# Diagonal steps ahead of the split of e, and Gram results formed from the first chunk to the third

## What is computed

```python
q = heads(hidden_states @ W_q)
probs_t = softmax(q @ heads(text_ehs @ W_k) * attn_scale)
text_out = probs_t @ heads(text_ehs @ W_v)
qsem = l2norm(einsum('bhst,bte->bhse', probs_t, text_ehs))
sem = einsum('bhse,bne->bhsn', qsem, l2norm(ip_ehs))
probs_ip = softmax(q @ heads(ip_ehs @ W_k_ip) * attn_scale + SEM_SCALE * sem) * spatial_mask
out = (text_out + probs_ip @ heads(ip_ehs @ W_v_ip)) @ W_out + b_out + hidden_states
```

## Time and profile before

| | us |
|---|---|
| median of 3 runs | 390.13 |
| lowest and highest | 387.19, 395.4 |
| the profiled execution | 389.0 |
| its span, first to last instruction | 387.0 |
| TensorE busy in it | 358.2 |
| mean granted TensorE clock | 0.974 of full |

### The profile page before, as it was taken

How to read it: one execution, slowest core, us unless ns; L and a number is a source line. 1 busy time by engine, 2 the same in 40 slices (tenths; PEclk the granted TensorE clock), 3 DMA queues, 4 the chain that set the end, 5 groups by cost and what they waited for, 6 DMA issues and landing times.

```text
span 387.0 us, 9366 instructions
## 1 busy us (share of the span) xinstructions
PE 358.2 (93%) x3498; PEld 304.9 (79%) x3498; DVE 269.1 (70%) x566; ACT 215.7 (56%) x490; POOL 213.1 (55%) x230
## 2 busy tenths in 40 slices
PE   8999799995899979999899979998999899999886
PEld 7879599874788868888788878886888678877664
DVE  4897673693667695587858685687758587867464
ACT  6734133783557455647556554757455458557741
POOL 8020271397138861596438662696349615865872
PEclk9999999998799989999999989999999999999899
DMA  8999993259105802265205702283203710002001
GB/s 265 313 240 188 249 188 105 64 169 157 23 1 158 155 13 59 81 142 103 75 5 176 134 22 65 82 179 63 77 3 103 128 42 3 2 3 58 0 3 31
DMA packets 30145, 38.01 MB, mean 98 GB/s; under 512 B 14394, under 2 KB 27307, under 8 KB 29419
## 3 DMA queue, kind: packets, MB, share of 16 engines
q1 hardware_dynamic: 29732, 37.00, 41.1%
q10 hardware_dynamic: 368, 0.41, 0.3%
HBM read 28.49 MB, written 8.81 MB: 96 GB/s over the span
## 4 chain that ended last, share of the span: by engine, by line
PE 64%; DVE 16%; DMA 9%; issue 6%; SPq 3%; ACT 1%; POOL 0%; DVEq 0%; ACTq 0%
PE PR L1127 32%; PE Y L1127 18%; PE O L1127 7%; PE P L1127 5%; DVE mx L1001 4%; DMA qst<-ma 3%; DVE dl L974 3%; DMA tri<-tri_d 2%; DMA big<-xT 2%; DVE pb L1025 2%; DVE ssq L885 1%; DMA kd<-ks 1%; PE PR L1326 1%; DVE cTl L1101 1%; SPq L519 1%
## 5 line engine op out<-in xcount | busy, mean ns | idle before, releaser
L633 POOL TENSOR_TENSOR pb<-pb 128x448 f32<-128x448 f32 x78 | 91.2, 1170 | 99.9 <-DVE pb L1025 96.9
L1001 DVE TENSOR_REDUCE mx<-PR 112x1 f32<-112x371 f32 x160 | 81.6, 536 | 50.5 <-PE PR L1127 49.5
L1025 DVE TENSOR_TENSOR pb<-big,Y 128x448 f32<-128x448 f32 x120 | 73.5, 617 | 32.1 <-PE Y L1127 30.5
L813 ACT ACTIVATE big<-P 128x448 f32<-128x448 f32 x120 | 64.7, 539 | 55.0 <-PE P L1127 55.0
L1127 PE MATMUL Y<-er,Gh 128*128 128x448 f32 x240 | 93.4, 413 | 1.7 <-ACT er L817 1.4
L817 ACT ACTIVATE er<-big 128x448 fp32r<-128x448 f32 x120 | 69.4, 578 | 3.8
L1127 PE MATMUL P<-qst,kst 99*128 99x112 bf16 x480 | 44.0, 218 | 9.4 <-DMA qst<-ma 9.0
L1127 PEld LDWEIGHTS Y<-er,Gh 128*128 128x128 f32 x240 | 46.1, 192 | 8.0 <-issue 2.3
L1127 PE MATMUL PR<-kst,qst 96*112 96x371 bf16 x160 | 48.7, 329 | 2.5 <-DVE mx L1001 2.1
L1127 PEld LDWEIGHTS P<-qst,kst 99*128 99x128 bf16 x480 | 30.6, 101 | 25.1 <-issue 17.8
L1127 PE MATMUL Y<-er,Gl 128*128 128x448 f32 x120 | 44.4, 370 | 0.0
(11 more groups left out here) (208 smaller groups left out, 719.1 us busy)
## 6 DMA issues: line engine op xcount, KB each, us to landing
et<-ctxT SPq DMA_DIRECT2D x7, 752.0 KB, 4.9
kst<-kd SPq DMA_DIRECT2D x7, 720.0 KB, 7.4
kd<-ks SPq DMA_DIRECT2D x16, 288.0 KB, 2.9
qst<-qd SPq DMA_DIRECT2D x48, 70.0 KB, 3.5
kst<-kd SPq DMA_DIRECT2D x7, 480.0 KB, 9.5
kst<-kd SPq DMA_DIRECT2D x9, 240.0 KB, 9.1
qd<-kst SPq DMA_DIRECT2D x4, 336.0 KB, 7.8
vx<-xr SPq DMA_DIRECT2D x8, 140.0 KB, 2.5
```

Of the source, the lines that this page charges most:

```text
L633: pool.tensor_tensor(total, total, (pz, pm)[j], ALU.add).then_inc(s_S, 1)
L813: act.activation(e, P[(3 * g + c) % 2][:, 0:448], ACT.Exp).then_inc(s_exp, 1)
L1001: dve.tensor_reduce(mx[b % 2][:, h:h + 1], bank[0:S, 0:T], AX.X, ALU.max).then_inc(s_free[seq[u] % NR], 1)
L1025: dve.tensor_tensor((pz, pm, pa[g % 2])[j], eb[g % 3][:, 448 * j:448 * j + 448], Y[y % 2][:, 0:448], ALU.mult).then_inc(s_P, 1)
```

## The change

The order of the words, and what goes with it. Grams run 0, 1, 2: each waits for its own chunk of `er`, the product of gram 0 goes to `pa`, and GpSimd adds after grams 1 and 2. In the middle batches `E` is cut in `Ea` and `Eb`, which stand behind `g1`, so that GpSimd takes gram 1's addition ahead of `el`; `g2` stands behind `o`. In `LATE`, `D` follows `pT`, and `S0` stands behind `cT` and `L`. In the start, `D` and `L` of batch 0 come behind the first maxima. `wo` and `Kr` of batch 0 come one and two rounds sooner; `D` of batch 1 ends round 3 instead of standing in round 4.

```diff
-ROUNDS = ("K0 S0 m g2 m g1 S1 m K1 m S2 m g0 v G0",
-          "S0 m g2 g1 m S1 m g0 K2 C v m S2 G1 m",
-          "S0 m g2 T0 T1 g1 m g0 r0 S1 m pw S2 m v V0 m",
-          "Kr r1 m g2 g1 S0 m m g0 V1 S1 m m S2 v r2 mT z GV",
-          "p g2 pT E g1 D cT S0 S1 v g0 L o S2")
-SECOND = "S0 K0 m g2 g1 m S1 m g0 K1 m v S2 m G0"
-NO_K = "m m S0 g2 m g1 v g0 S1 S2 m m G0"
-EARLY = ("m S1- m S2- K1 S0 m g2 g1 S1 m m g0 m S2 K2",
-         "S0 m g2 g1 S1 m g0 S2 m v m m wo C",
-         "S0 m g2 g1 m S1 g0 m m S2 v m",
-         "Kr S0 m S1 m g2 m g1 m v g0 S2 mT GV",
-         "E g2 g1 S0 g0 D v S1 S2 L")
-LATE = "p g2 pT g1 S0 g0 D cT S1 L S2 v o"
-LAST = ("S0 S1 v g2 S2 g1 T0 T1 g0",
-        "S0 r0 g2 g1 pw v S1 g0 pv S2",
-        "S0 r1 g2 S1 r2 g1 g0 S2 v",
-        "S0 g2 S1 z g1 p g0 S2 v",
-        "pT T0' pw' r0' g2 cT g1 g0 r1' v vW T1' r2' pv'")
+ROUNDS = ("K0 m S0 m g0 g1 S1 m K1 S2 m g2 m v G0",
+          "g0 S0 m m g1 g2 S1 m m K2 C v S2 G1 m",
+          "Kr S0 m g0 m T0 T1 g1 g2 S1 r0 pw m S2 m v V0",
+          "m g0 g1 S0 m r1 m m g2 V1 S1 m S2 m v r2 mT z GV",
+          "p g0 pT g1 Ea Eb D cT S0 S1 v L S2 o g2")
+SECOND = "K0 S0 m K1 g0 g1 m S1 m v g2 m S2 m G0"
+NO_K = "m m S0 S1 g0 m g1 v m g2 S2 m G0"
+EARLY = ("m S1- m S2- K1 S0 g0 g1 S1 m S2 m g2 K2 m wo",
+         "m m g0 S0 g1 S1 m g2 S2 m v m m C Kr",
+         "g0 S0 m g1 m S1 g2 m m S2 v m",
+         "S0 m S1 g0 m m g1 m v g2 S2 mT GV D",
+         "Ea Eb g0 g1 v S0 S1 g2 S2 L")
+LATE = "p g0 pT D g1 g2 cT L S0 S1 v S2 o"
+LAST = ("S0 v g0 S1 g1 T0 g2 S2 T1",
+        "g0 r0 S0 g1 v pw S1 g2 pv S2",
+        "r1 S0 S1 g0 g1 r2 g2 S2 v",
+        "S0 g0 S1 g1 z p S2 g2 v vW",
+        "pT T0' g0 r0' pw' cT g1 g2 r1' v T1' r2' pv'")
@@ master_schedule, the start
-    order += [("D", 0)]
-    side = [("V", 0, 1), ("L", 0), ("V", 0, 2)] + [("qip", b) for b in range(B)]
+    side = [("V", 0, 1), ("D", 0), ("V", 0, 2), ("L", 0)] + [("qip", b) for b in range(B)]
@@ master_schedule, the words
-                elif w == "E":
-                    order += split(b + 3) if b + 3 < B else []
+                elif w in ("Ea", "Eb"):
+                    order += split(b + 3)[2 * (w == "Eb"):][:2] if b + 3 < B else []
@@ GpSimd
-                if u[0] == "gram" and u[2] < 2 and u[1] < NG * B - 1:
+                if u[0] == "gram" and u[2] and u[1] < NG * B - 1:
                     g, j = u[1], u[2]
                     total = pa[g % 2]
-                    pool.wait_ge(s_P, 3 * g + 3 - j)
-                    if j == 0:
+                    pool.wait_ge(s_P, 3 * g + j + 1)
+                    if j == 2:
                         pool.wait_ge(s_S, 2 * g + 1)
-                    pool.tensor_tensor(total, total, (pz, pm)[j], ALU.add).then_inc(s_S, 1)
+                    pool.tensor_tensor(total, total, (pm, pz)[j - 1], ALU.add).then_inc(s_S, 1)
@@ VectorE
-                    y = 3 * g + 2 - j
+                    y = 3 * g + j
                     dve.wait_ge(s_gram, y + 1)
-                    if j == 2 and g >= 2:
+                    if j == 0 and g >= 2:
                         dve.wait_ge(s_pv, g - 1)
-                    if j < 2 and g:
-                        dve.wait_ge(s_S, 2 * g - j)
-                    dve.tensor_tensor((pz, pm, pa[g % 2])[j], eb[g % 3][:, 448 * j:448 * j + 448], Y[y % 2][:, 0:448],
+                    if j and g:
+                        dve.wait_ge(s_S, 2 * g - 2 + j)
+                    dve.tensor_tensor((pa[g % 2], pm, pz)[j], eb[g % 3][:, 448 * j:448 * j + 448], Y[y % 2][:, 0:448],
                                       ALU.mult).then_inc(s_P, 1)
@@ TensorE
-                    y = 3 * g + 2 - j
+                    y = 3 * g + j
                     if y >= 2:
                         pe.wait_ge(s_P, y - 1)
-                    if j == 2 and r == 0:
+                    if j == 0 and r == 0:
                         pe.wait_ge(s_wd, b + 1)
-                    if j == 2:
-                        pe.wait_ge(s_er, 3 * g + 3)
+                    pe.wait_ge(s_er, 3 * g + j + 1)
```

More of the change, by code:

```diff
@@ L125, in master_schedule @@
                 if w == "g":
-                    order += [("gram", g, j) for j in (2, 1, 0)]
+                    order += [("gram", g, j) for j in range(3)]
                 elif w in ("g2", "g1", "g0"):
```

## The result

| | before | after |
|---|---|---|
| median, us | 389.68 | 371.02 |
| lowest and highest | 387.19, 395.4 | 370.6, 371.63 |
| the profiled execution | 389.0 | 370.6 |
| its span | 387.0 | 368.6 |
| TensorE busy | 358.2 | 352.1 |

A forecast was written before the change was run, and what follows sets the result against it. TensorE, busy for 93% of the span, was taken as the bound, leaving waits and lost clock to win. 4.5 + 3.4 + 2.3 + 2.0 + 0.4 + 1.2 - 0.5 = 13.3 us, so 377 us for the median, range 370 to 386.

The forecast's parts named there:

- the likeliest case: Whole kernel: the gains come as summed, 377 us, with its own range 371 to 382; chance 0.65.
- What bounds it, and `el`: Round 4, batches 1 to 4: `el` behind the diagonal steps removes the wait for `cTl` before `o`, 6.86 us.
- Given back to `St`: Batches 1 to 4: `St` chunk 0 waits for `ma` with less cover, 0.6 us lost each, between 0 and 0.8.
- The clock: Batches 1 to 4: two stretches of half clock behind waits before `o` go, 3.4 us, bounds 0 and 3.4.
- Batches 5 and 6: Late order: `St` chunk 0 behind gram 2, `cT` and `L` shortens its wait; 2.3 us, bounds 1.0 and 2.6.
- The start: Batch 0's start: three reductions go ahead of `D`, which waited for `tri`; 2.0 us, bounds 0 and 3.0.
- Batch 0: Batch 0: the earlier `wo` split lets the k load and `ma` start sooner; 0.4 us, bounds -0.5 and 1.5.
- Batch 7 and the grams: Last batch: with grams first to third, gram 2's 1.37 us wait for `er` shrinks; 1.2 us, bounds 0 and 2.9.
- `el` later: Batches 1 to 4: `el` ends later, close to K's need; 0.5 us lost in all, bounds 0 and 4 x 0.8.
- (a): Rival: the wait moves to `St` chunk 0, the clock falls as often, the start gives nothing; 383.7 us, chance 0.22.
- (b): Rival: GpSimd's queue is the limit, its second addition comes last and `pv` waits for it; 387 us, chance 0.08.
- (c): Rival: slower than before, `el` meets `L`'s two instructions, K waits and the clock falls; 391 us, chance 0.05.

The follow-up runs named there:

- a_late_back: The changed kernel with the old order of words in `LATE` (batches 5 and 6), grams first to third; median 374.0 us, ratio 0.958 to the kernel before.
- a_el_ahead: The changed kernel with `el` put back ahead of gram 1 in round 4, all else kept; median 383.7 us, ratio 0.980 to the kernel before.
- b_start: The kernel before with only the start changed, `D` and `L` of batch 0 behind the first maxima; ratio 0.992 to the kernel before.
- a_same: The changed kernel again, unaltered, on another chip; 371.08 us, ratio 0.953 to the kernel before.
- b_gram_up: The kernel before with only the grams turned, `g0` and `g2` changing places in every string of words; ratio 1.021 to the kernel before, 8 us slower.
- a_last_back: The changed kernel with the old words of `LAST` in batch 7, grams first to third; median 373.3 us, ratio 0.959 to the kernel before.
- a_plus: The changed kernel with three more words moved, gram 1 in round 2 of middle batches, `K2` and gram 1 in batch 0; median 372.5 us, ratio 0.955.

## Why the prediction was right, point by point

The measured 371.0 lies inside the range of 370 to 386, but 1 us above its low end and at the edge of the 371 to 382 of the likeliest case; the single value was 377. The main mechanism, `el` beside the diagonal steps, was right. The range held although several terms were off, and with little more than 1 us of gain on top it would not have held.

**What bounds it, and `el`.** Right, and near to the tenth. I gave the diagonal steps 1.97 us, they took 1.96; `cTl` was to end 7.0 us behind `mT` and ended 7.03 behind it; the whole wait in front of `o` went. Moving `el` alone, and moving it back alone, both show that this is the cause.

**Given back to `St`: the step was wrong.** I took 0.6 us in each batch, because `St` chunk 0 waits for `ma` behind the k load. After, `St` starts 5.24 to 5.34 us behind `mT` in batches 1 to 4 and never waits. I had taken the k load's place as fixed, since moving `Kr` does nothing in these batches. That sentence was right, but K's own products come sooner in the new order of round 1: in batch 3 the load was issued 217.81 - 211.54 = 6.3 us ahead of `mT`, and 208.32 - 200.34 = 8.0 after:

```profile
200.34 1.27 SPq L419 DMA_DIRECT2D kst<-kd  x3
...
208.97 2.47 SPq L518 DMA_DIRECT2D qst<-ma  x3
```

A queue that never waits for TensorE still follows the instruction that feeds it. The writes of k were issued 10.6 us ahead of `mT` before and 11.9 after. The sooner load isn't the whole of it: in batch 2 it was issued 6.6 us ahead of `mT` after, and `St` did not wait, where in batch 4 before it was issued 6.7 us ahead and `St` waited until 6.3 us behind `mT`. What else lets `ma` land sooner stays open. The term was 2.4 us too large.

**The clock.** The mechanism is right: fill the waits with matmuls and the clock stays up. The size was the larger miss. I counted the two stretches of batches 1 to 4, 3.4 us, and those came through. I put the clock at nothing in the start, in batch 0 and in batch 7. In the profiled executions all but 3.4 of the 20.5 us at half clock went, and TensorE's busy time fell by 6.1 us. The rule by which I chose, that waits of 1.4 us leave the clock alone, was drawn from two cases. In a_late_back a wait of 1.38 us had half clock behind it; in a_el_ahead one of 1.86 had none, in b_start those of 1.96 and 2.05 had none, and of the 2.52 and 2.80 us in batch 0 of the changed kernel the longer, in a_same, had none. So the length of the last wait alone doesn't decide it. What else does stays open; with less idle time in all there were fewer stretches.

**Batches 5 and 6.** 2.3 us forecast, and 2.5 measured up to `mT` 7, for batch 5 alone; batch 6's share lies in the last column, where its wait of 0.55 us went. Undone, it costs 3.

**The start.** 2.0 us forecast, 2.8 in the profiled execution, 2.2 in b_start and 1.6 in a_same. VectorE is indeed the limit afterwards, and directly only 1.1 us came through; the rest is the half clock at 46.7 and the moment at which the clock first rose. That the term came out near is in part luck.

**Batch 0.** 0.4 us forecast, 2.5 measured. The load was to start up to 1.5 us sooner and I took 0.8 of it; by the timelines it was issued 88.17 - 84.40 = 3.8 us ahead of `mT` before and 5.9 after, 2.2 sooner, and with it the wait fell by 2.8 us. Here, too, the step that failed is that K's products were taken to stay in place: the writes of k were issued 8.9 us ahead of `mT` before and 10.2 after.

**Batch 7 and the grams.** 1.2 us forecast, some 2 measured, for another reason than mine. I had it that gram 2's wait for `er` goes, and that turning the grams costs nothing in the middle, its work being the same. b_gram_up shows that the turn alone costs 8 us, half clock included. a_last_back, turned but with the old words, loses the 2 us again, 1.5 of them by half clock, which I had left out of the term. That the change as a whole did not pay for it I got right without seeing why.

**`el` later.** 0.5 us forecast, nothing measured. `el` was to end 10.7 us behind `mT` and ended 10.05 behind it; K came 9.57 behind it and read the second half in time. The rule of the Trainium skill on VectorE and GpSimd ("SBUF — State Buffer", "Who interferes with whom") agrees with the trace in what it would do here: the first of `L`'s two instructions takes 2.11 us instead of 0.59. It costs nothing where nothing waits, as after, and 1.5 us in four batches where three maxima do, as in a_plus.

**The rivals.** (a), the wait moves, did not come: `St` never waited in batches 1 to 6, and the clock did not fall as often. (b) and (c) did not come either. b_gram_up is near to (b), but the queue that was too slow was VectorE's, with its products, and not GpSimd's.

**The sum by stages.** Forecast against measured, in us: the start 2.0 and 2.8, batch 0 0.4 and 2.5, batches 1 to 4 4.5 + 3.4 - 0.5 = 7.4 and 8.6, the rest 2.3 + 1.2 = 3.5 and 2.5 + 2.1 = 4.6. Every stage gave more than its term in the profiled executions, 5.1 us in all. Two steps lie behind much of that: the clock was put at nothing outside batches 1 to 4, and K's place was taken as fixed.

## What to carry to other kernels

An instruction that comes out several times its usual length on VectorE is worth a look at what GpSimd does beside it; which of the two goes first is a matter of one word in the order, and here worth half of a 4.6% gain. A wait of TensorE can cost more than its length, since half clock may follow it: count the stretches of half clock and put them in the sum, with a range, since they come and go between executions of the same kernel. An order of the work and the spacing of its words belong together; turned by itself, the order of the changed kernel was the slower one.

## What the runs showed of the hardware

- An instruction of VectorE that GpSimd holds up can be served between two instructions of GpSimd: `dl` (0.55 us) went ahead of the second piece of `el`, 2.08 us in all, and not some 4. So did the product of 20 columns in the changed kernel: it takes 0.60 us instead of 0.22 before, and ends between two additions on GpSimd. It isn't always so: in a_plus the same product, 1.86 us, was not served between the two rows of GpSimd shown there, but behind the second.
- With 1.84 to 1.86 us of idle TensorE in an otherwise full stretch, the clock fell to half in three cases of four, for 3.4 us, and took some 1.6 us each time. With matmuls of no use in the same places it fell in none of four. The length of the wait alone does not decide: 1.96 and 2.05 us in b_start had no half clock behind them, 1.95 and 2.06 us in the kernel before had.
- Small transfers behind large ones on the same queue: `ma` is three transfers of 4.4 KB. `St`, which reads them, started 5.2 us behind `mT` without a wait where the k load was issued 8.0 us ahead of it. Where it was 5.1 to 6.7 us ahead `St` waited in some batches of the kernel before, until 6.3 to 6.7 us behind `mT`, and in others not; after, with 6.6 us, it did not.
